# Audio tower on one core: late weight pieces split during sampling and attention, and every sixth half tile of the first mixture summed by ScalarE

## The reference

```python
h = tokens(x)                                   # 500 frames -> 166 tokens of 128
h = h + linear_recurrence(layernorm(h))         # L0 attn: complex diagonal recurrence
h = h + first_mixture(layernorm(h))             # L0 ffn, below
h = h + sparse_attention(layernorm(h))          # L1 attn: 25..42 sampled keys choose the queries
h = h + second_mixture(layernorm(h))            # L1 ffn: 64 experts, top 42, gelu

# first_mixture: 16 experts, top 2, hidden 512; only the mean over an expert's tokens is used
hidden = silu(einsum('td,efd->tef', x, w1))
h_sum  = einsum('tef,te->ef', hidden, mask)     # sum over the tokens that chose the expert
y_mean = einsum('ef,edf->ed', h_sum / counts, w2)
out    = einsum('tk,tkd->td', routing_w, y_mean[top_idx])
```

## Time and profile before

| what | value |
|---|---|
| median of three runs | 2065.45 us (2064.77 to 2066.51) |
| the profiled execution | 2067.39 us; from first to last instruction 2065.7 us |
| granted PE clock, mean | 0.939 |
| first mixture, its first matmul to its last sum | 283.3 to 397.6 us |
| tail of the mixture | 397.6 to 428.9 us |
| norm 3 until the first diagonal reaches PE | 428.9 to 455.9 us |
| projections and sampling | 455.9 to 583.9 us |
| attention | 583.9 to 716.9 us |
| second mixture | 716.9 to 2065.7 us |
| busy: PE, DVE, POOL, ACT | 91%, 81%, 70%, 67% |

### The profile page before, as it was taken

How to read it: one execution, slowest core, us unless ns; L and a number is a source line. 1 busy time by engine, 2 the same in 40 slices (tenths; PEclk the granted TensorE clock), 3 DMA queues, 4 the chain that set the end, 5 groups by cost and what they waited for, 6 DMA issues and landing times.

```text
span 2065.7 us, 50535 instructions
## 1 busy us (share of the span) xinstructions
PE 1870.1 (91%) x17038; PEld 1349.7 (65%) x17038; DVE 1676.4 (81%) x4833; ACT 1378.0 (67%) x2149; POOL 1455.0 (70%) x1098
## 2 busy tenths in 40 slices
PE   7887436789989978999999999999999999999998
PEld 5555213456669855777777777777777777777776
DVE  5887736555678788899999999999999999999998
ACT  4134525424435545888888888888888888888886
POOL 2216679559800032888888888888888888888887
PEclk9998768789989965999999999999999999999999
DMA  3011289523200010000000200000100000000000
GB/s 93 21 35 63 81 246 257 124 67 94 90 1 1 22 63 1 2 2 0 0 0 3 82 2 0 0 0 35 49 1 0 0 0 2 2 10 11 10 11 19
DMA packets 64334, 77.56 MB, mean 38 GB/s; under 512 B 38932, under 2 KB 47028, under 8 KB 62132
## 3 DMA queue, kind: packets, MB, share of 16 engines
q1 hardware_dynamic: 61364, 70.08, 11.7%
q0 software_dynamic: 2816, 5.45, 0.8%
HBM read 42.97 MB, written 24.08 MB: 32 GB/s over the span
## 4 chain that ended last, share of the span: by engine, by line
PE 58%; DVE 3%; issue 2%; ACT 1%; POOL 0%; ACTq 0%; DVEq 0%; POOLq 0%
PE bank L2679 30%; PE bank L2662 28%; DVE m_work L2553 1%; DVE m_best L2550 1%; DVE m_work L2544 0%; PE bank L2632 0%; DVE m_ut L1269 0%; ACT m_h L2485 0%; DVE m_best L2543 0%; DVE m_ex L2555 0%; DVE h L2591 0%; DVE m_red L2556 0%; DVE m_row L2536 0%; POOL m_diag L1255 0%; ACT m_hidden L2482 0%
## 5 line engine op out<-in xcount | busy, mean ns | idle before, releaser
L2679 PEld LDWEIGHTS bank<-weights,m_h 128*128 128x128 f16 x10752 | 649.6, 98 | 194.4 <-DVE hc L2582 82.6
L2430 POOL TENSOR_TENSOR m_h<-m_hidden,m_h 128x896 f16<-128x896 f32 x384 | 725.9, 1890 | 32.0
L2679 PE MATMUL bank<-weights,m_h 128*128 128x128 f16 x10752 | 724.6, 219 | 10.7 <-POOL m_h L2430 2.1
L2582 DVE SCALAR_TENSOR_TENSOR hc<-bank,m_shares,hc 128x128 f32<-128x128 f32 x2688 | 727.2, 342 | 4.3 <-PE bank L2679 4.3
L2482 ACT ACTIVATE m_hidden<-bank,m_b 128x896 f32<-128x896 f32 x384 | 386.9, 1007 | 197.6 <-PE bank L2662 197.5
L2567 DVE TENSOR_TENSOR m_h<-bank,m_h 128x896 f16<-128x896 f32 x384 | 419.2, 1092 | 116.8 <-ACT m_h L2485 116.7
L2428 POOL TENSOR_SCALAR m_h<-m_hidden 128x896 f16<-128x896 f32 x384 | 360.8, 939 | 117.9 <-ACT m_hidden L2482 99.5
L2662 PE MATMUL bank<-m_u_first,weights 128*128 128x448 f16 (+1 forms) x1536 | 417.8, 354 | 5.5 <-DVE h L2591 5.5
L2662 PE MATMUL bank<-m_u_second,weights 128*128 128x448 f16 (+1 forms) x1536 | 417.7, 354 | 0.0
L2479 ACT ACTIVATE bank<-bank,m_b 128x896 f32<-128x896 f32 x384 | 377.6, 983 | 0.6 <-PE bank L2662 0.6
L2485 ACT ACTIVATE m_h<-bank 128x896 f16<-128x896 f32 x384 | 349.1, 909 | 0.0
(11 more groups left out here) (359 smaller groups left out, 2153.9 us busy)
## 6 DMA issues: line engine op xcount, KB each, us to landing
weights<-expert_factors SPq DMA_DIRECT2D x12, 1024.0 KB, 8.8
lru_w_in<-e_w_dram SPq DMA_DIRECT2D x16, 512.0 KB, 4.5
expert_factors<-lru_w_out SPq DMA_DIRECT2D x16, 512.0 KB, 4.3
ew_raw<-e_w_dram SPq DMA_DIRECT2D x16, 512.0 KB, 3.9
weights<-w_dram SPq DMA_DIRECT2D x16, 256.0 KB, 2.8
weights<-w_dram SPq DMA_DIRECT2D x4, 1024.0 KB, 6.6
expert_factors<-ew_made SPq DMA_DIRECT2D x8, 512.0 KB, 3.0
xs<-x_dram SPq DMA_DIRECT2D x4, 996.0 KB, 11.8
```

What stands on the lines that cost most here:

```text
L2430: g.tensor_tensor(h1[:, x, 1], hidden[:, x], h1[:, x, 0], ALU.subtract).then_inc(second_of[1], 1)
L2582: last = v.scalar_tensor_tensor(acc[:, m * TW:(m + 1) * TW], y[q][:, (n - start) * TW:(n - start + 1) * TW], shares[:, m, e:e + 1], acc[:, ...
L2679: last = t.matmul(y[q][:, (n - start) * TW:(n - start + 1) * TW], factors[:, m, n * TW:(n + 1) * TW], k.weights[:, grp % 2, 2 + m, at], st ...
```

## The change

Two edits.

First, class `LateWeights` is gone. The sampling block now splits pieces 0 to 15 and the attention block pieces 16 to 31; all go through the code of `ExpertWeights` (POOL L2216 to L2224 in the new numbering, where `pool_diagonal` is L1254). The wait until all stores have landed moves from the end of the sampling block's SP stream to the end of the attention block's.

Second, half tiles 5, 11, 17, ... of the first mixture (14 of 86) are summed by ACT: in place of one SiLU over 128x768 ACT issues two over 128x384, each with `accum_out` into its column of `part`, and DVE skips them. PE waits for `silu` there in place of `summed`.

```diff
-    KEEP_FROM, KEEP_EVERY = 4, 5
+    BY_ACT = 6
+    def act_sums(self, n):
+        return n % self.BY_ACT == self.BY_ACT - 1
+    def dve_sets(self, n):
+        return n - n // self.BY_ACT
+    def wait_summed(self, eng, n):
+        if self.act_sums(n):
+            eng.wait_ge(self.silu, n + 1)
+        else:
+            eng.wait_ge(self.summed, self.dve_sets(n + 1))
...
     def sync(self, sp, outputs_made):
-        late.sync_load(sp, 0)
-        late.sync_load(sp, 1)
...
-            if j >= self.KEEP_FROM and (j - self.KEEP_FROM) % self.KEEP_EVERY in (0, 2):
-                late.sync_keep(sp)
-        while late.kept < late.count:
-            late.sync_keep(sp)
-        late.sync_kept(sp)
...
-    def pool(self, pool):
-        for i in range(self.late.count):
-            self.late.pool_piece(pool, i)
...
     def act(self, act):
             act.wait_ge(self.up, j + 1)
-            self.nc.scalar.activation(self.set_banks(j), self.set_banks(j), ACT.Silu).then_inc(self.silu, 1)
+            if self.act_sums(j):
+                for f in range(self.FP):
+                    at = j % self.PARTS * self.FP + f
+                    last = self.nc.scalar.activation(self.set_banks(j)[:, f], self.set_banks(j)[:, f], ACT.Silu,
+                                                     accum_out=self.part[:, j // self.PARTS, at:at + 1])
+            else:
+                last = self.nc.scalar.activation(self.set_banks(j), self.set_banks(j), ACT.Silu)
+            last.then_inc(self.silu, 1)
     def dve(self, dve):
         for j in range(PARTS * NST):
+            if self.act_sums(j):
+                continue
             dve.wait_ge(self.silu, j + 1)
...
                 if f % FP == 0 and n >= SETS:
-                    pe.wait_ge(self.summed, n - SETS + 1)
+                    self.wait_summed(pe, n - SETS)
...
             def _(sp):
-                k.expert_weights.sync_pieces(sp, *PIECES_N3)
                 k.expert_weights.sync_pieces(sp, *PIECES_SAMPLE)
             def _(pool):
-                k.expert_weights.pool_pieces(pool, *PIECES_N3)
                 first, end = PIECES_SAMPLE
                 for c in range(NC):
                     norm.pool_diagonal(pool, c, c % 2, stats)
-                    if 1 <= c <= end - first:
+                    if c:
                         k.expert_weights.pool_pieces(pool, first + c - 1, first + c)
+                k.expert_weights.pool_pieces(pool, first + NC - 1, end)
...
+        @block.sync
+        def _(sp):
+            k.expert_weights.sync_pieces(sp, *PIECES_ATTEND)
+        @block.gpsimd
+        def _(pool):
+            k.expert_weights.pool_pieces(pool, *PIECES_ATTEND)
...
-PIECES_N3, PIECES_SAMPLE, PIECES_SENDING = (0, 3), (3, 2 * GROUP), (2 * GROUP, NG * GROUP)
+PIECES_SAMPLE, PIECES_ATTEND = (0, 2 * GROUP), (2 * GROUP, NG * GROUP)
...
-        if end == 2 * GROUP:
+        if end == NG * GROUP:
             for p in range(2):
-                sp.wait_ge(self.k.kept_out[p], 16 * GROUP // 2)
+                sp.wait_ge(self.k.kept_out[p], 16 * (NG - 1) * GROUP // 2)
```

More of the change, by code:

```diff
@@ L937, in recurrence @@
         routing.begin(ctx, on_diag[:], tables.work[:], va[:], raw_room)
-        mixture = FirstMixture(nc, k, routing, w_in[:], w_out[:], ut[:], state_of[:], xc[:], xsn[:])
+        mixture = FirstMixture(nc, k, routing, ut[:], state_of[:], xc[:], xsn[:])
         diag_ready = sem("diag_ready")
@@ L992, in _ @@
             mixture.pool_clear(pool)
-            mixture.pool(pool)
         @block.scalar
@@ L1281, with __init__ @@
     W2_AT = (3, 8, 13)
-    KEEP_FROM, KEEP_EVERY = 4, 5
-    def __init__(self, nc, k, routing, w_in, w_out, ut, state_of, xc, xsn):
+    BY_ACT = 6
[8 more added lines that the diff above has]
+            eng.wait_ge(self.summed, self.dve_sets(n + 1))
+    def __init__(self, nc, k, routing, ut, state_of, xc, xsn):
         def sem(name):
@@ L1289, in __init__ @@
         states = state_of.rearrange("p a b c d e -> p (a b c d e)")
-        self.late = LateWeights(nc, k, w_in.rearrange("p a b c d -> p (a b c d)").rearrange("p (j n) -> p j n", j=2),
-                                w_out.rearrange("p a b c d -> p (a b c d)")[:, 0:2 * PIECE].bitcast(F16).rearrange("p (j q n) -> p j q n", j=2, q=2),
-                                states[:, 0:PIECE])
-        self.hsum = states[:, PIECE:PIECE + FC * E0 * E0].rearrange("p (f x) -> p f x", f=FC)
-        self.ym = states[:, PIECE + FC * E0 * E0:PIECE + FC * E0 * E0 + 128]
+        self.hsum = states[:, 0:FC * E0 * E0].rearrange("p (f x) -> p f x", f=FC)
+        self.ym = states[:, FC * E0 * E0:FC * E0 * E0 + 128]
         self.part = xc.rearrange("p q c -> p (q c)")[:, 0:NST * FC].rearrange("p (n f) -> p n f", f=FC)
@@ L1329, in sync @@
     def sync(self, sp, outputs_made):
-        k, routing, late = self.k, self.routing, self.late
+        k, routing = self.k, self.routing
         sp.wait_ge(outputs_made, NC)
-        late.sync_load(sp, 0)
-        late.sync_load(sp, 1)
         sp.wait_ge(k.w0_split, NC)
@@ L1407, in pe @@
         pe.wait_ge(k.w2_in, 16 * 4)
-        pe.wait_ge(self.summed, PARTS * NST)
+        pe.wait_ge(self.silu, PARTS * NST)
+        pe.wait_ge(self.summed, self.dve_sets(PARTS * NST))
         for f in range(FC):
@@ L2210, in pool_pieces @@
             g.tensor_tensor(out[:, 1], left, out[:, 0], ALU.add).then_inc(self.split, 1)
-class LateWeights:
-    def __init__(self, nc, k, raw, made, left):
-        self.nc, self.k = nc, k
-        self.raw, self.made, self.left = raw, made, left
-        self.raw_in = [k.semaphore(f"lw_raw_in{p}") for p in range(2)]
-        self.kept_out = [k.semaphore(f"lw_kept_out{p}") for p in range(2)]
-        self.rounded = k.semaphore("lw_rounded")
-        self.raw_read = k.semaphore("lw_raw_read")
-        self.widened = k.semaphore("lw_widened")
-        self.split = k.semaphore("lw_split")
-        self.first, self.end = PIECES_SENDING
-        self.count = self.end - self.first
-        self.kept = 0
-    def sync_load(self, sp, i):
-        if i >= self.count:
-            return
-        n = self.first + i
-        src = self.k.a["e_w1"] if n % GROUP < PIECES else self.k.a["e_w2"]
-        if i >= 2:
-            sp.wait_ge(self.raw_read, i - 1)
-        first = n // GROUP * GE * HC * 128 + n % PIECES * PIECE
-        sp.dma_start(self.raw[:, i % 2, :], src[:, first:first + PIECE]).then_inc(self.raw_in[i % 2], 16)
-    def sync_keep(self, sp):
-        i = self.kept
-        if i >= self.count:
-            return
-        n = self.first + i
-        mat, cols = n % GROUP // PIECES, slice(n % PIECES * PIECE, (n % PIECES + 1) * PIECE)
-        self.sync_load(sp, i + 2)
-        sp.wait_ge(self.split, i + 1)
-        sp.dma_start(self.k.kept[n // GROUP - 1, :, 2 * mat:2 * mat + 2, cols], self.made[:, i % 2]).then_inc(self.kept_out[i % 2], 16)
-        self.kept += 1
-    def sync_kept(self, sp):
-        for p in range(2):
-            sp.wait_ge(self.kept_out[p], 16 * self.count // 2)
-    def pool_piece(self, pool, i):
-        g, j = self.nc.gpsimd, i % 2
-        raw, left, out = self.raw[:, j], self.left, self.made[:, j]
-        pool.wait_ge(self.raw_in[j], 16 * (i // 2 + 1))
-        if i >= 2:
-            pool.wait_ge(self.kept_out[j], 16 * (i // 2))
-        g.tensor_copy(out[:, 0], raw).then_inc(self.rounded, 1)
-        pool.wait_ge(self.rounded, i + 1)
-        if i:
-            pool.wait_ge(self.split, i)
-        g.tensor_tensor(left, raw, out[:, 0], ALU.subtract).then_inc(self.raw_read, 1)
-        pool.wait_ge(self.raw_read, i + 1)
-        g.tensor_scalar(left, left, 1.0 / SHARE, 1.0, ALU.mult, ALU.mult).then_inc(self.widened, 1)
-        pool.wait_ge(self.widened, i + 1)
-        g.tensor_tensor(out[:, 1], left, out[:, 0], ALU.add).then_inc(self.split, 1)
```

## The result

The changed kernel takes 2069.85 us, the median of 20 runs (2066.02 to 2074.12), against 2064.35 for the kernel before (20 runs, 2062.63 to 2066.96 and one at 2081.94): a ratio of 1.0023, with a 95% interval of 1.0014 to 1.0033. It is slower, by about 5.5 us. I had forecast 2063.0, no change; the time lies inside the range of 2050 to 2083, on the side to which I gave 0.33.

A forecast was written before the change was run, and what follows sets the result against it. The mixture was taken as DMA bound by late-piece traffic. Loop -42, tail -2, norm 3 and sampling start -10.5, attention +52 sum to -2.5: 2063.0 us as median, own range 2052 to 2073, 2050 to 2083 overall.

The forecast's parts named there:

- the sum of the loop: First mixture's loop: ACT the limit by a little once late pieces go, 72 us against 114.3, -42.
- its term: Attention: four DVE instructions a sequence each wait out a POOL instruction, +52 us, bounds 45 and 66.
- the prediction's other price for it: Mixture's loop: by the skill's ACTIVATE price ACT's pair costs about 0.9 us, loop DVE bound at 4.35, some 3 less.
- The tail: Tail of the first mixture: PE from a busy loop starts at full clock, -2 us, bounds 0 and -4.
- the wait of 5.0: Start of sampling: PE's wait for POOL before its first spread goes, -5.0 us.
- the holds of 3.6: Norm 3's statistics: DVE instructions no longer held by POOL's pieces, -3.6 us.
- The 2.4 for the clock: Norm 3 and start of sampling: with the waits gone, PE's half clock at 460 to 464 gives 2.4 us back.
- the cover: Sampling: POOL's three more pieces and tables end near 570.5, before the stage's 573.4, so hidden by some 3 us.
- the 17 piece times of the sum: Attention: 16 sequences of pieces plus one piece time for number-step holds, 7.05 us each, 17th sequence beginning at 120.
- rivals one and three: Attention: DVE pairs pass together, about +20, time 2031 (0.12); or the sequence falls out of step, +70, 2081 (0.13).
- the second: Attention: DVE is not held by POOL there, +0, time 2011; chance 0.05.
- The fourth: First mixture: PE's clock stays low, loop 88 us, -26 in place of -42, time 2079; chance 0.12.

The follow-up runs named there:

- e2: Changed kernel with all 86 half tiles summed by DVE, so only the weight pieces are moved: 2071.69 us.
- e4: Kernel before with only the second edit, 14 of 86 half tiles summed by ACT: 2068.0 us, ratio to before 1.0012.
- e1: Changed kernel with PE reading all 43 expert numbers into registers before its first tile: 2054.75 us, ratio to before 0.995.
- e5: Changed kernel with POOL's index tables and masks made at the start of the sampling block: 2064.66 us.
- e3: Changed kernel without POOL's instructions in attention, loads, stores and handshakes kept, pieces 16 to 31 not split: 2022.73 us.
- e15: Kernel before with one sentinel memset written in two parts, one POOL instruction more: 2053.88 us.

## Why the prediction was right or wrong

Up to the second mixture, my terms came to -2.5 and the profiles show +11.4; the second mixture then gave 12.3 that I had put at nothing. Two errors of opposite sign nearly met. That the time came within 7 us of the forecast is luck, and the sign came out wrong. The step that failed is the sum of the loop: it put at nothing PE's stalls for its registers, 12.7 us, and with them it would have been -29. Next to it, sampling's loss of 4 had been counted as hidden. What made up for both was the attention, 8 under its term, and the second mixture's 12.3, for which there was no term.

The profiles differ by -1.1 where the medians differ by +5.5; the traces of the other runs place 4.4 of these 6.6 us (2.2 in the loop, 1.1 in the second mixture, 0.7 in attention and 0.4 in sampling, by the means of the traces with the same stage, e2 left out), and the rest is not placed.

- **The mixture's loop: the limit was right, a stall was missing.** DMA bound before (e4), ACT and DVE bound after at 4.6 to 4.8 for six. ACT's pair costs about 0.97 us, by the start of the next row in its timeline, against my 1.05. (At the prediction's other price for it, 0.9, ACT would be the limit as well, 3.5 + 0.9 = 4.4 against DVE's 4.35; the prediction says DVE.) But the sum counted only engines and queues. PE's reads of 16 and 11 registers stood in the trace before as "issue" waits, 5.58 and 4.35 us at tiles 16 and 32, and no term named them; I took them for part of the tile waits that would go. They cost 12.7 us with the restart at half clock (e1).
- **The tail**: -1.0 for -2; the clock was 0.50 again from 371 to 374, after PE had stood 2.10 us for the last sums.
- **Norm 3**: the wait of 5.0 and the holds of 3.6 went as forecast (-8.2 of -8.6). The 2.4 for the clock did not come: it was 0.50 from 420 to 424 as it had been from 460 to 464 in the second of the earlier trace rows.
- **Sampling: the cover was measured at the wrong end.** I asked whether POOL ends before the stage, and it did. The chain that mattered was DVE's choice step some 16 us before the stage's end, whose instructions are of the kind that is held. That cost 4 (e5 gives 5.2 back).
- **Attention: the mechanism was right, the size 8 too large.** I added DVE's own time to each piece, but POOL does not slow down. The likely reason, argued and not shown by itself, is that it takes its turn while DVE works from PSUM or waits. The period is the piece, 6.55 and not 7.05, and the 17 piece times of the sum at 0.5 less each are 8.5 us. The 17th sequence began 109.9 us into the stage, not 120. The pairs did not pass together, nor did the sequence fall out of step: rivals one and three are out, and so is the second, since L1963 and L1993 took three to four times as long while POOL worked and fell back without it (e3). The fourth, which the bounds of the loop call the third, named 88 for the loop, and 86.9 came, but not for its reason: the clock was 0.89, low after the two stalls, and 0.98 without them (e1). The lock that the Trainium skill's page "SBUF — State Buffer", section "SBUF: two separate sides", states fits the holds read here: a held instruction ends 0.02 to 0.2 us after the one of POOL that it waited for. My words narrowed it too far: the page asks that the GpSimd instruction read SBUF only where DVE has two SBUF inputs, and the memset, which reads nothing, held a cast for 2.50 us, while the addition L1492 beside it, with two SBUF inputs, kept its 0.33 (e2).
- **The second mixture** was taken as unchanged because its code is. That is a step without a row, and it was worth 12.3 us in the profiles. That a single POOL instruction can give as much (e15, one run, 1335.8 us for the stage) shows that code around it matters; the cause isn't settled.
- **The range** of 2052 to 2073 is narrower than its terms: their bounds, simply added, give 2046 to 2088, and the working doesn't say how they were taken together.

## What to carry to other kernels

Work moved to an idle engine is not free if the engine's instructions are long and a neighbour has instructions that wait for them: count the neighbour's instructions that are held, one at a time, and shorten the moved ones. Ask of every "issue" wait in front of the engine that will be the limit whether it is really part of the wait that goes. And before trusting half a per cent, look at stages whose code is the same: their length can move with the program around them.

## What the runs showed of the hardware

- Hold times grow with the length of POOL's instruction: a sequence of attention lost 2.95 us with 128x1024, 1.9 with 128x512 and 0.7 with 128x256 instructions, at a POOL that was busy all the time.
- While PE read 16 register values no matmul started for 5.20 us (5.58 in the kernel before), and while it read 11 for 4.22 (4.35). Read ahead of the first tile, in a wait of 35 us, they cost nothing (e1).
- POOL's memset, which reads nothing, held a DVE cast for 2.50 us (e2). A reciprocal over 2 columns from SBUF to SBUF was not held in any sequence (0.15 to 0.17 us).
- A SiLU over 128x384 with accumulator takes 0.48 us and its read 0.19, and two of them follow one another at 0.46 to 0.50.
